# A graph-attention layer: one merged edge and one-hot product per group, a TensorE loop without register work, and a scratch write on Pool at every second group

## The chip, the cores and the metric

The kernel runs on one core of a Trainium2 chip. The metric is the device time of one execution, in microseconds (us); lower is better. Three runs of the kernel before gave 4992.13, 4989.86 and 4984.16 us, with a median of 4989.86 us.

## The reference

There are 12500 nodes with 128 features and 412500 edges with 64 features, sorted by their `dst`. Cut to what matters:

```python
h = x @ Wn + bn ; q = x @ Wq + bq ; k = x @ Wk + bk ; v = x @ Wv + bv
eh = edge_attr @ We + be
attn_in = concatenate([q[src], k[dst], eh], -1)          # per edge
hmid = leaky_relu(attn_in @ A1 + b1, 0.2)
scores = leaky_relu(hmid @ A2 + b2, 0.2)                 # 8 heads
w = softmax(scores.mean(-1), axis=0)                     # over all edges
out = segment_sum(w[:, None] * v[dst], src)
y = layernorm(h + out) * gamma + beta
result = layernorm(x + y)
```

## The kernel before

`attn_in @ A1` is split in three: a product of the source node, one of the destination node and one of the edge's features. The table phase (25 chunks of 512 nodes) computes the two node products for all nodes. The source products (`pq`) go to a table in memory (`pq_dram`). The destination products (`pk`) stay in the on-chip memory as a sum of three bf16 tables (high, middle, low), which ScalarE (L581, L586), VectorE (L811) and Pool (L495) make.

The main loop then goes over the edges in 403 pairs of groups; a group is 512 edges, so there are 806 groups. The weights of the softmax are needed only at the end, and nearly all of them are zero there, so the tail handles only tiles with weights above zero. In the main loop each group passes these steps:

- Pool gathers the source products of the group's edges with four indirect DMAs of 128 rows (L500), into one of 8 slots of `rows`. Before it gathers into a slot again, it waits until TensorE has used it (`s_added`, L514).
- SyncE loads `dst` and the edges' features of a pair (L402, L405), two pairs ahead of their use at most.
- VectorE compares `dst` with a window of 128 nodes, which gives a one-hot matrix in bf16 (L909).
- TensorE forms in one PSUM bank the product of the edges' features (fp32, L724), adds three bf16 products of the one-hot matrix with the three tables (L733), whose place in `pk` a register gives, and adds the gathered rows by four transposes (L713). A group whose edges cross into the next window of 128 nodes gets three more products (L744) in a loop behind an `If`.
- The last transpose raises `s_added`. ScalarE scales the bank (L612), VectorE takes the maximum (L926, the leaky relu), and TensorE multiplies the result by the head weights (L692, fp32). This product is called `score_mm`, and it stands behind the next group's products in TensorE's order.
- For every four groups ScalarE and VectorE apply the heads' leaky relu (L604, L933), TensorE transposes the heads (L700) and VectorE sums them to scores (L940).

In the first half of the main loop, each second pair also handles a block of 128 nodes: a product on TensorE (L763) and two layer norms on VectorE.

The order of the work on each engine is written out by hand in `pair_step` and `node_step` of each engine; `over_pairs` loops over them with four pairs in a turn. Where a step needs the number of its window or the count of further windows, its engine loads it from the table `info` into a register (`info_of`, L328) and works on it with register instructions (L731, L733, L736). TensorE's own piece of this for each group is

```python
word = word_of(pe, g)                                   # L729, one load per pair
first, more = window_of(word, h)                        # L730
pe.wait_ge(s_onehot, g + 1)
for c in range(3):                                      # L733
    pe.matmul(to, flat[:, bass.ds(first * (3 * P) + c * P, P)], onehot[:, h, :], ...)
with pe.If(more > 0): ...
```

Of the kernel before, what the change touches and what calls it, by code (L numbers as in the profile page):

```python
# [22 lines left out]
EXTRA = 1  # L43
QUAD = 4
SLOPE = 0.2
EPS = 1e-5
MORE = 256
# [4 lines left out]
FIRST_PAIRS = 3  # L52
FIRST = 2 * FIRST_PAIRS
TURN_PAIRS = 4
RING = 2 * TURN_PAIRS
SRC_RING = 4
# [6 lines left out]
def over_pairs(eng, pairs, blocks, pair_step, node_step):  # L63


    for q in range(FIRST_PAIRS):
        pair_step(q, q % 2, q // 2, None, 0)
    total = (pairs - FIRST_PAIRS) // TURN_PAIRS
    assert total * TURN_PAIRS + FIRST_PAIRS == pairs
    halves = TURN_PAIRS // 2  # L70
    with_nodes = -(-(blocks + BLOCK_LAG) // halves)
    peel = -(-BLOCK_LAG // halves)
    full = blocks // halves
    assert total > with_nodes + 1 and full > peel

    def iteration(i, nodes):
        for u in range(TURN_PAIRS):
            n = FIRST_PAIRS + u
            pair_step(n + TURN_PAIRS * i, n % 2, n // 2 + halves * i, u, i)
            if nodes:  # L80
                node_step(halves * i + u // 2, u % 2)

    for i in range(peel):
        iteration(i, True)
    with eng.Fori(peel, full) as i:
        iteration(i, True)
    for i in range(full, with_nodes):
        iteration(i, True)
    with eng.Fori(with_nodes, total - 1) as i:
        iteration(i, False)  # L90
    iteration(total - 1, False)
# [8 lines left out]
def build(nc, x_rows, x_blocks, x_chunks, edges, src_first, src_ring, dst_pairs, dst_spans, src_tiles, dst_tiles, wqT, wkT, weT, wv, wn,  # L100
          bn, bq, bk, bv, be, A1, b1, A2, b2, gamma, beta, out, n_edges):
# [9 lines left out]
    assert chunks * CW == n_pad and D == P and 2 * DE == P and tiles < KEY and blocks <= MORE and n_pad <= 1 << 16  # L111
    info_parts = P
    info_cols = dst_spans.shape[1] // GROUP
    turns = (pairs - FIRST_PAIRS) // TURN_PAIRS
    assert info_parts * info_cols >= groups and turns * TURN_PAIRS + FIRST_PAIRS == pairs
    assert (turns - SRC_RING) % SRC_RING == 0 and info_cols + 8 < chunks
# [3 lines left out]
    pq_dram = nc.dram_tensor("pq_dram", (n_pad, D), F32).ap()  # L120
    y_dram = nc.dram_tensor("y_dram", (n_pad + P, D), F32).ap()
# [1043 lines left out]
```

## Time and profile before

| | before |
|---|---|
| median of three runs | 4989.86 us |
| the profiled execution, its own time | 4998.4 us |
| its span, from the first to the last instruction | 4996.5 us |
| TensorE (PE) busy | 3236.5 us, 65% |
| Pool busy | 3095.7 us, 62% |
| VectorE (DVE) busy | 1407.0 us, 28% |
| ScalarE (ACT) busy | 736.6 us, 15% |
| mean granted TensorE clock | 0.798 of full speed |
| mean busy share of the 16 DMA engines | about a third in the main loop |

No engine is busy for more than two thirds of the span. A busy share doesn't tell what an engine waits for between its instructions; for that, the rows below show idle time with what ended it. "Remote" and "another core or an unknown queue" stand where the profile could not tie the end of a wait to a recorded instruction; with one core in use there is no other core. In a row of a group of instructions, the first number after the bar is the group's busy time, the second the mean duration of one in ns; after the second bar stands the idle time of the engine just before them.

### The profile page before, as it was taken

To read this page: it belongs to the slowest core of one execution; us is meant where nothing else is said; L and a number is where in the kernel's file an instruction comes from. 1 tells how busy PE (TensorE), PEld (TensorE's weight loads), DVE (VectorE), ACT (ScalarE), POOL (GpSimd) and SP (SyncE) were. 2 spreads that over 40 slices of the span, in tenths; PEclk is the share of its full clock that TensorE was granted. 3 is DMA by queue.
4 is the path that set the end of the run, shared out by engine and by line. 5 is a ranking of instruction groups with operands and counts; after the bars stand their busy time and mean duration, and the time that the engine had idled before them with its cause. 6 is when DMAs were issued, how large, how long until landed. Compare 5 with 4: busy or idle time off the path is not lost.

```text
span 4996.5 us, 58367 instructions
## 1 busy us (share of the span) xinstructions
PE 3236.5 (65%) x10213; PEld 1586.8 (32%) x10416; DVE 1407.0 (28%) x3449; ACT 736.6 (15%) x1268; POOL 3095.7 (62%) x3270
## 2 busy tenths in 40 slices
PE   5566666666666666676666666666666666666665
PEld 3233333333333333333333323333333332333332
DVE  4233333333333333333332222222222222222223
ACT  2111111111111111111111111111111111111111
POOL 5566666666666666666666666666666666666663
PEclk8788778788777878878788787877777788877787
DMA  5333333333333333333333333333333333333332
GB/s 159 88 98 98 98 96 100 97 98 99 96 100 96 97 96 102 96 96 100 98 96 89 88 85 90 89 88 87 90 85 86 90 87 88 88 86 88 88 88 60
DMA packets 311865, 467.39 MB, mean 94 GB/s; under 512 B 88001, under 2 KB 153665, under 8 KB 311698
## 3 DMA queue, kind: packets, MB, share of 16 engines
q1 hardware_dynamic: 207138, 254.92, 17.1%
q0 software_dynamic: 103328, 211.82, 16.3%
q10 hardware_dynamic: 1360, 0.20, 0.0%
q8 instruction: 15, 0.25, 0.0%
q14 instruction: 24, 0.20, 0.0%
HBM read 446.78 MB, written 19.86 MB: 93 GB/s over the span
## 4 chain that ended last, share of the span: by engine, by line
another core or an unknown queue 39%; PE 29%; issue 20%; ACT 5%; DVE 5%; DVEq 2%; ACTq 0%; DMA 0%; SPq 0%; POOL 0%; POOLq 0%
PE banks L692 9%; PE banks L724 7%; PE banks L733 5%; PE banks L713 5%; ACT sloped L612 3%; DVE hidden L926 3%; ACT head_s L604 1%; PE banks L744 1%; PE banks L700 1%; DVEq L328 1%; DVE onehot L909 0%; DVEq L97 0%; DVEq L909 0%; ACT node_m L621 0%
## 5 line engine op out<-in xcount | busy, mean ns | idle before, releaser
L500 POOL DMA_INDIRECT rows<-pq_dram,src_i x3200 | 3032.3, 948 | 1799.3 <-issue 929.9
L692 PE MATMUL banks<-hidden,a_wide 128*128 128x512 f32 x1612 | 1101.0, 772 | 1101.5 <-DVE hidden L926 1021.6
L926 DVE SCALAR_TENSOR_TENSOR hidden<-banks,bias_col,sloped 128x512 f32<-128x512 f32 x806 | 604.8, 750 | 2867.4 <-ACT sloped L612 2229.2
L612 ACT ACTIVATE sloped<-banks,bias_col 128x512 f32<-128x512 f32 x806 | 540.2, 686 | 4009.1 <-remote 2387.4
L724 PE MATMUL banks<-edge,w_fold 128*128 128x512 f32 x1612 | 1017.5, 719 | 42.8 <-issue 21.6
L733 PE MATMUL banks<-onehot,pk 128*128 128x512 bf16 x2216 | 714.9, 428 | 307.9 <-issue 187.6
L692 PEld LDWEIGHTS banks<-hidden,a_wide 128*128 128x128 f32 x1612 | 300.5, 233 | 1179.3 <-DVE hidden L926 1087.4
L713 PE MATMUL banks<-ident,rows 128*128 128x128 f32 x3224 | 551.8, 299 | 132.7 <-issue 131.4
L733 PEld LDWEIGHTS banks<-onehot,pk 128*128 x2418 | 264.5, 109 | 1039.0 <-issue 969.4
L713 PEld LDWEIGHTS banks<-ident,rows 128*128 128x128 f32 x3224 | 449.5, 157 | 347.3 <-issue 241.2
L724 PEld LDWEIGHTS banks<-edge,w_fold 128*128 128x128 f32 x1612 | 361.2, 236 | 442.3 <-issue 420.7
L909 DVE TENSOR_SCALAR onehot<-dst_b,iota_f 128x512 bf16<-128x512 uint16 x806 | 295.8, 367 | 80.0 <-issue 63.1
L744 PE MATMUL banks<-extra,pk 128*128 128x512 bf16 x291 | 101.2, 434 | 128.9 <-issue 114.2
L700 PEld LDWEIGHTS banks<-ident,head_l 128*128 128x128 f32 x808 | 126.2, 170 | 153.6 <-issue 151.8
L700 PE MATMUL banks<-ident,head_l 128*128 128x128 f32 x808 | 152.1, 322 | 2.8 <-issue 1.7
L933 DVE SCALAR_TENSOR_TENSOR head_l<-banks,b_cols,head_s 128x512 f32<-128x512 f32 x202 | 150.1, 743 | 7.7 <-issue 7.7
L604 ACT ACTIVATE head_s<-banks,b_cols 128x512 f32<-128x512 f32 x202 | 138.0, 683 | 2.7 <-PE banks L692 2.7
L940 DVE TENSOR_REDUCE score<-banks 128x128 f32 (+1 forms) x202 | 57.5, 285 | 267.3 <-remote 208.9
L744 PEld LDWEIGHTS banks<-extra,pk 128*128 x291 | 30.2, 104 | 192.2 <-issue 175.7
L621 ACT ACTIVATE node_m<-node_m,cols 128x1 f32<-128x1 f32 x200 | 58.4, 292 | 176.1 <-issue 120.4
L917 DVE TENSOR_SCALAR extra<-dst_b,iota_f 128x512 bf16<-128x512 uint16 x97 | 35.3, 364 | 167.6 <-issue 167.6
L658 PE MATMUL banks<-w_fold,xa 128*128 128x256 f32 x200 | 48.7, 397 | 10.4 <-DVE w_fold L803 5.1
(133 smaller groups left out, 630.5 us busy)
## 6 DMA issues: line engine op xcount, KB each, us to landing
dst_b<-in_dst_pairs_dram SPq DMA_DIRECT2D x403, 256.0 KB
edge<-in_edges_dram SPq DMA_DIRECT2D x403, 256.0 KB
rows<-pq_dram,src_i POOLq DMA_INDIRECT x3200
xa<-in_x_chunks_dram SPq DMA_DIRECT2D x25, 256.0 KB, 3.3
pq_dram<-rows SPq DMA_DIRECT2D x25, 256.0 KB, 3.0
node_x<-in_x_blocks_dram SPq DMA_DIRECT2D x100, 64.0 KB
node_r<-in_x_rows_dram SPq DMA_DIRECT2D x100, 64.0 KB
y_dram<-node_y SPq DMA_DIRECT2D x100, 64.0 KB
```

What stands on the lines that cost most here:

```text
L500: pool.indirect_dma_start(to, None, pq_dram, bass.IndirectOffsetOnAxis(at, 0)).then_inc(s, 16)
L604: act.activation(head_s[:, :], heads[slot], ACT.Identity, bias=b2_cols[:, 1:2], scale=SLOPE).then_inc(s_head_s, 1)
L612: act.activation(sloped[:, h, :], pre[2 * slot + h], ACT.Identity, bias=bias_col[:, 1:2], scale=SLOPE).then_inc(s_sloped, 1)
L692: pe.matmul(heads[slot], a2_wide[:, j, :], hidden[:, j, :], start=(j == 0), stop=(j == QUAD - 1 or last), skip_group_check=True).then_inc( ...
L700: last = pe.transpose(turned[:, k * P:(k + 1) * P], head_l[:, k * P:(k + 1) * P], ident[:, :])
L713: last = pe.matmul(pre[2 * slot + h][:, k * P:(k + 1) * P], four[k], ident[:, :], is_transpose=True, start=False, stop=(k == TILES - 1), s ...
L724: product = pe.matmul(to, w_fold[:, 2 + h, :], edge[:, slot, :], start=True, stop=False, skip_group_check=True)
L733: last = pe.matmul(to, flat[:, bass.ds(first * (3 * P) + c * P, P)], onehot[:, h, :], start=False, stop=False, skip_group_check=True)
L744: last = pe.matmul(to, flat[:, bass.ds(at, P)], extra[:, w, :], start=False, stop=False, skip_group_check=True)
L909: dve.tensor_scalar(onehot[:, h, :], dst, iota_f[:, bass.ds(first, 1)], None, ALU.is_equal).then_inc(s_onehot, 1)
L926: dve.scalar_tensor_tensor(out=hidden[:, j, :], in0=pre[j], scalar=bias_col[:, 0:1], in1=sloped[:, h, :], op0=ALU.add, op1=ALU.max).then_i ...
L933: dve.scalar_tensor_tensor(out=head_l[:, :], in0=heads[slot], scalar=b2_cols[:, 0:1], in1=head_s[:, :], op0=ALU.add, op1=ALU.max).then_inc ...
```

## The change

1. **Windows of 64 nodes from the pair's first `dst`.** The destination products stay in fp32 and are written to memory (`pk_dram`) in five pieces at the end of the table phase. For each pair SyncE loads the 64 rows of `pk_dram` that begin at the pair's lowest `dst` into the first 64 partitions of `window_w`, whose other 64 partitions hold the edge weights. The steps that made three bf16 tables are gone, Pool's L495 with them.
2. **One product.** VectorE writes the one-hot matrix as fp32 into the first 64 partitions of `moving` (one instruction of 1024 words for a pair); the edges' features are loaded into the other 64. One fp32 product of 128 rows per group gives both parts. The products of the former L733 and L744 are gone. Further windows are handled only if a pair spans more than 64 nodes.
3. **TensorE's loop.** The loop counter counts in steps of 64, and the semaphores that TensorE waits on count in the same steps, so that the waits compare with the counter itself. Buffers have fixed places. One load (the count of further windows in a turn) is left per turn of eight pairs, and one branch per pair.
4. **Order.** The pre-activation products of both groups of a pair come first, then both groups' transposes, then the head products of the pair before. ScalarE and VectorE work on both groups of a pair. Heads are collected over 16 groups in place of four.
5. **Pool.** The ring of gathered rows has 16 slots in place of 8. After every second group's gathers Pool writes 512 words per partition of the scratch tile `pace` (`pause`).
6. **SyncE.** It loads four pairs ahead, when `s_added` tells that the pair in the same slot is done.

The diff, cut to its core:

```diff
+TURN_PAIRS = 8
+PACE = 512
+PACED = 2
+RING = 2 * TURN_PAIRS
+AHEAD = 4
+SHOWN = 2
...
@@ SyncE
+            for k in range(PK_PARTS):
+                sp.wait_ge(s_pk, chunks // PK_PARTS * (k + 1))
+                sp.dma_start(pk_dram[...], pk_blocks[...]).then_inc(s_pk_out, 16)
...
+            sp.wait_ge(s_pk_out, 16 * PK_PARTS)
+            def pair_load(p, slot):
+                at = word(sp, base, p, n_pad - WINDOW)
+                sp.dma_start(window_w[0:WINDOW, slot, :], pk_dram[bass.ds(at, WINDOW), :]).then_inc(s_pair[slot], 16)
+                sp.dma_start(dst_b[:, slot, :],
+                             dst_pairs[bass.ds(p, 1), :].to_broadcast([WINDOW, PAIR])).then_inc(s_pair[slot], 16)
+                sp.dma_start(moving[WINDOW:P, 2 * slot:2 * slot + 2, :]..., edges[bass.ds(p, 1), :, :]...)
...
+                        sp.wait_ge(s_added, 2 * n + 2)
+                        pair_load(n + AHEAD, u % AHEAD)
@@ Pool
-            for c in range(chunks):
-                pool.wait_ge(s_pk_mid, c + 1)
-                pool.tensor_tensor(pk[..., 2, :], ..., ALU.subtract).then_inc(s_pk_lo, 1)
+            def pause(n):
+                wait(pool, s_paced, n)
+                pool.sem_inc(s_passed, 1)
+                pool.memset(pace[:, :], 0.0).then_inc(s_paced, 1)
             def turn(i, w, later, of=RING):
                 pool.wait_ge(s_src[w], ...)
                 for r in range(of):
                     if not isinstance(i, int) or i > 0:
-                        pool.wait_ge(s_added, FIRST + RING * i + r - RING + 1)
+                        pool.wait_ge(s_added, RING * i + r - RING + 1)
                         pool.sem_inc(s_passed, 1)
                     for k in range(TILES):
                         gather(rows[:, r, k, :], src_i[:, w, at:at + 1], s_rows[r])
+                    if r % PACED == PACED - 1:
+                        pause(RING // PACED * i + r // PACED)
@@ TensorE
+            def pair_step(u, tick):
+                first, slot = 2 * (u % 2), u % AHEAD
+                if u == 0:
+                    more[0] = word(pe, more_i, tick >> TICK_BITS, windows)
+                pe.wait_ge(s_onehot[u], tick)
+                for h in range(2):
+                    pe.matmul(pre[first + h], window_w[:, slot, :], moving[:, 2 * slot + h, :], start=True, ...)
+                with pe.If(more[0] > 0):
+                    ...
+                for h in range(2):
+                    pe.wait_ge(s_rows[2 * u + h], tick)
+                    for k in range(TILES):
+                        last = pe.matmul(pre[first + h][...], rows[:, 2 * u + h, k, :], ident[:, :], is_transpose=True, ...)
+                    last.then_inc(s_added, 1)
+                if u > 0:
+                    heads_of_pair(u - 1, tick)
...
+            def heads_of_pair(u, tick, last_pair=False):
+                pe.wait_ge(s_hidden[u], tick)
+                for h in range(2):
+                    last = pe.matmul(heads, a2_wide[:, 2 * u + h, :], hidden[:, 2 * (u % 2) + h, :], ...)
@@ VectorE
+            def show(p, slot, s, loaded):
+                dve.wait_ge(s_pair[slot], loaded)
+                dve.tensor_scalar(moving[0:WINDOW, 2 * slot:2 * slot + 2, :]...,
+                                  dst_b[:, slot, :], base_f[:, bass.ds(p, 1)], None, ALU.is_equal).then_inc(s, TICK)
```

## Rows read from the trace of the kernel before

**Rows 1.** From the page: busy us (share of the span) and instructions of each engine.
```profile
PE 3236.5 (65%) x10213; PEld 1586.8 (32%) x10416; DVE 1407.0 (28%) x3449; ACT 736.6 (15%) x1268; POOL 3095.7 (62%) x3270
```
**Rows 2.** The chain that ended last, by engine, from the page.
```profile
another core or an unknown queue 39%; PE 29%; issue 20%; ACT 5%; DVE 5%; DVEq 2%; ACTq 0%; DMA 0%; SPq 0%; POOL 0%; POOLq 0%
```
**Rows 3.** Waits: engine line, who ended them: us in total, times, longest.
```profile
ACT sloped L612 <- remote: 2387.4, 258, 28.1
ACT sloped L612 <- PE banks L713: 1050.1, 222, 14.4
...
POOL rows L500 <- remote: 721.9, 241, 3.9
...
POOL rows L500 <- PE banks L713: 147.5, 78, 4.4
```
**Rows 4.** Timeline of ScalarE from 85 to 175 us: start, duration, what, idle before.
```profile
128.68 0.69 ACT L612 ACTIVATE sloped<-banks,bias_col 128x512 f32<-128x512 f32 x1 [28.08 <-remote]
156.01 0.69 ACT L612 ACTIVATE sloped<-banks,bias_col 128x512 f32<-128x512 f32 x1 [26.64 <-remote]
```
**Rows 5.** Timeline of TensorE's products in the same stretch.
```profile
106.26 0.60 PE L713 MATMUL banks<-ident,rows 128*128 128x128 f32 x4
...
134.30 0.60 PE L713 MATMUL banks<-ident,rows 128*128 128x128 f32 x4
```
**Rows 6.** Timeline of Pool: first gather, end of the first run, last gather.
```profile
79.92 1.29 POOL L500 DMA_INDIRECT rows<-pq_dram,src  x1 [3.04 <-DMA pq_dram<-rows]
...
149.16 0.94 POOL L500 DMA_INDIRECT rows<-pq_dram,src_i  x1 [0.30 <-issue]
165.80 0.95 POOL L500 DMA_INDIRECT rows<-pq_dram,src_i  x1 [15.69 <-issue]
...
4940.79 0.95 POOL L500 DMA_INDIRECT rows<-pq_dram,src_i  x1 [0.30 <-issue]
```
**Rows 7.** Timeline from 4028 to 4050 us: one run of Pool, and ScalarE behind it.
```profile
4029.89 0.96 POOL L500 DMA_INDIRECT rows<-pq_dram,src_i  x1 [3.71 <-remote]
...
4038.57 0.60 PE L713 MATMUL banks<-ident,rows 128*128 128x128 f32 x4
...
4043.66 0.94 POOL L500 DMA_INDIRECT rows<-pq_dram,src_i  x1 [0.30 <-issue]
...
4047.21 0.69 ACT L612 ACTIVATE sloped<-banks,bias_col 128x512 f32<-128x512 f32 x1 [9.36 <-remote]
4047.96 0.94 POOL L500 DMA_INDIRECT rows<-pq_dram,src_i  x1 [3.35 <-remote]
```
**Rows 8.** Line L500, all gathers in the ring: duration ns min/median/max, first and last start.
```profile
L500 POOL DMA_INDIRECT rows<-pq_dram,src_i x3200: 941/947/1101, 110.4 to 4940.8; - x189
```
**Rows 9.** Pool's scratch and constant writes, from the groups by line.
```profile
L481 POOL MEMSET ones_f<- 128x128 f32 x1 | 0.2, 195 | 0.0
...
L483 POOL MEMSET ones_b<- 128x1 bf16 x1 | 0.1, 92 | 0.0
```
**Rows 10.** Chain from 157 to 163 us: start, us, what; half clock, then full clock.
```profile
157.54 2.08 PE banks L692 x2
...
162.22 0.86 PE banks L692 x2
163.08 0.86 PE banks L724 x2
163.94 0.65 PE banks L733 x3
164.59 0.44 PE banks L713 x4
```
**Rows 11.** Groups by line: ScalarE's scaling and VectorE's one-hot matrix.
```profile
L612 ACT ACTIVATE sloped<-banks,bias_col 128x512 f32<-128x512 f32 x806 | 540.2, 686 | 4009.1 <-remote 2387.4 <-PE banks L713 1050.1 <-issue 563.5
...
L909 DVE TENSOR_SCALAR onehot<-dst_b,iota_f 128x512 bf16<-128x512 uint16 x806 | 295.8, 367 | 80.0 <-issue 63.1 <-DMA dst_b<-in_dst_pairs_dram 9.8 <-remote 7.0
```
**Rows 12.** Line L733, TensorE's register instructions: duration ns min/median/max, first and last start.
```profile
L733 PEldq FUSED_REGOPS  x2418: 3/46/1419, 87.9 to 4954.5; - x186
```

More of the change, by code:

```diff
@@ L451, in _ @@
-            for j in range(full, with_nodes):
-                four_turns(j, True)
-            with sp.Fori(with_nodes, fours - 1) as j:
-                four_turns(j, False)
-            four_turns(fours - 1, False)
+            for p in range(AHEAD):
+                pair_load(p, p)
+            with_nodes = 1 - (-(blocks + BLOCK_LAG) // (TURN_PAIRS // 2))
+            full = blocks // (TURN_PAIRS // 2)
+            turn(0, 0, False)
+            turn(1, 1, True)
+            with sp.Fori(1, full // SRC_RING) as j:
+                two_turns(j, True)
@@ L458, in _ @@
+            after = full // SRC_RING * SRC_RING
+            ends = -(-with_nodes // SRC_RING) * SRC_RING
+            for i in range(after, ends):
+                turn(i, i % SRC_RING, i < with_nodes)
+            with sp.Fori(ends // SRC_RING, turns // SRC_RING - 1) as j:
+                two_turns(j, False)
+            for i in range(turns - SRC_RING, turns):
+                turn(i, i % SRC_RING, False)
             sp.wait_ge(s_left, 1)
@@ L684, in _ @@
+            pe.wait_ge(s_window_e, 1)
+            pe.wait_ge(s_info, INFO)
             pe.sem_inc(s_extra_used, 1)
[L685 to L693 removed]
@@ L695, in heads_turn @@
-            def heads_turn(quad):
-                pe.wait_ge(s_head_l, quad + 1)
-                wait(pe, s_score, quad)
+            more = [None]
+            def heads_of_pair(u, tick, last_pair=False):
+                pe.wait_ge(s_hidden[u], tick)
+                if u == 0:
+                    pe.wait_ge(s_head_l, tick)
+                for h in range(2):
+                    g = 2 * u + h
+                    ends = g == RING - 1 or (last_pair and h == 1)
+                    last = pe.matmul(heads, a2_wide[:, g, :], hidden[:, 2 * (u % 2) + h, :], start=(g == 0), stop=ends,
+                                     skip_group_check=True)
+                    if ends:
+                        last.then_inc(s_heads, 1)
@@ L701, in heads_turn @@
                 last.then_inc(s_head_t, 1)
-            def add_rows(q, h, slot, u, i):
-                g = 2 * q + h
-                if isinstance(q, int) and q < FIRST_PAIRS:
-                    pe.wait_ge(s_rows_0[g], 64)
-                    four = [rows_0[:, g, k, :] for k in range(TILES)]
-                else:
-                    pe.wait_ge(s_rows[2 * u + h], 64 * (i + 1))
-                    four = [rows[:, 2 * u + h, k, :] for k in range(TILES)]
-                for k in range(TILES):
-                    last = pe.matmul(pre[2 * slot + h][:, k * P:(k + 1) * P], four[k], ident[:, :], is_transpose=True,
-                                     start=False, stop=(k == TILES - 1), skip_group_check=True)
-                last.then_inc(s_added, 1)
@@ new lines, in relu, with heads_relu @@
+            def relu(g, j, s):
+                dve.wait_ge(s_sloped, g + 1)
+                last = dve.scalar_tensor_tensor(out=hidden[:, j, :], in0=pre[j], scalar=bias_col[:, 0:1],
+                                                in1=sloped[:, j, :], op0=ALU.add, op1=ALU.max)
+                if s is not None:
+                    last.then_inc(s, TICK)
+            def heads_relu(batch):
+                dve.wait_ge(s_head_s, batch + 1)
+                dve.scalar_tensor_tensor(out=head_l, in0=heads, scalar=b2_cols[:, 0:1], in1=head_s, op0=ALU.add,
+                                         op1=ALU.max).then_inc(s_head_l, TICK)
```

712 lines of the change are left out of this document (329 added, 383 removed).

## The prediction, made before the changed kernel ran

> **What bounds the kernel now.** I read the busy shares first: no engine passes 65%, Pool has 62% [rows 1]. So the end is set by waits, and the chain that ended last says the same: 39% of it is a wait whose end the profile can't name, more than TensorE's own 29% [rows 2]. The list of waits says who stands in it: ScalarE waits 2387.4 + 1050.1 us for the bank that TensorE fills, and Pool waits 721.9 + 147.5 us in 319 stalls for slots of its ring [rows 3]. Both wait for one signal, `s_added`, raised by the last transpose of a group.
>
> The timeline shows that this signal comes late. TensorE's transposes of one group are recorded at 106.26 and end by 106.9; ScalarE, with nothing before it, starts on a bank only at 128.68. The transposes at 134.30 end by 134.9; the next start is at 156.01 [rows 4, 5]. Waits of 28.08 and 26.64 us, while TensorE does nothing that is recorded. What is special about this stretch is Pool: from 79.92 to 149.16 it issues 56 gathers without a gap above 0.3 us, then it has a full ring and stands still until 165.80 [rows 6]. After its stop the next signal comes within 6 us. In steady work the same is seen smaller: Pool issues 12 gathers from 4029.89 to 4043.66; transposes are recorded at 4038.57, but ScalarE starts only at 4047.21, after 9.36 us of idling and 2.6 us after Pool's last gather ended (4043.66 + 0.94 = 4044.60); Pool itself then stalls 3.35 us for the same signal [rows 7]. I read this as: while Pool issues gathers without a break, TensorE's signals are held back; Pool fills its ring, stops, and the signals pass. This reading is a correlation of rows. The other candidate is TensorE's own register work: three register instructions per group at L733 with a median of 46 ns but up to 1419 ns [rows 12].
>
> Pool is therefore the clock of the main loop, with stalls on top. One gather takes 947 ns (941 to 1101) [rows 8] and the next starts 0.30 us later [rows 6], so 1.25 us each. 806 groups x 4 = 3224 gathers x 1.25 = 4030 us. From the first gather to the end of the last, 4941.7 - 79.9 = 4861.8 us passed [rows 6]. The difference, 832 us, is stalls. This is all that a change which keeps the gathers can win in that stretch.
>
> **The change part by part.**
>
> *Products.* At full clock a group's parts on TensorE take 0.86 (head product), 0.86 (edges), 0.65 (three one-hot products) and 0.44 us (transposes) [rows 10]. The 0.65 goes; the merged product has the shape of the edge product and costs the same 0.86. Per pair that is 2 x 2.16 = 4.3 us at full clock; at half clock some 8.7 us, since one head product there takes 2.08 us with its start [rows 10] and I double the rest. Both lie under Pool's 10.0 us per pair, so this part is worth nothing by itself. It gives slack: 1.3 us per pair at full clock, and the group loops at L744 go.
>
> *TensorE's register work and order.* Before, each group is one round: signal, ScalarE 0.69 us [rows 11], VectorE, head product. After, a pair is one round, and its head products stand behind the next pair's products and transposes (2.6 us), which hide ScalarE's and VectorE's work. Register instructions fall away but for one load per eight pairs. Below: nothing; above: the whole 832 us, if they hold the signals. Either reading puts the gain in the same 832 us, so I count it once.
>
> *Pool's write.* 128 words take 195 ns and one word 92 ns [rows 9]: 0.81 ns a word, so 512 words take 0.51 us. The trace has no such write between gathers. Low end: it fills the 0.30 us between two gathers and costs 0.2. High end: it has such a gap on either side, 1.1. I take 0.65 us (the write and half a gap), nearest to the measured write. 403 x 0.65 = 262 us (81 to 443). In return Pool's runs are cut to 8 gathers, 10 us, where before they are 12 to 56. Waiting for the earlier write (`s_paced`) costs nothing: that is eight gathers old.
>
> *The ring of 16* lets Pool be up to 80 us ahead, so a late signal of 10 us no longer stops it, unless TensorE falls behind on average.
>
> *Table phase.* Pool's, ScalarE's and VectorE's extra passes go, the span reductions stay and a load and eight short steps move ahead; before, the first gather is at 79.92. I leave it there (70 to 90). SyncE stores 6.4 MB of destination products before the first pair is loaded, which delays TensorE, not Pool: its ring takes 64 gathers, 80 us, until it must wait. For the case that this cover is short I add one stall as at 165.80, about 20 us.
>
> *VectorE.* One write of 1024 words per pair in place of two of 367 ns [rows 11], 0.7 to 1.4 us, with two relus and the node work well under 10 us per pair; hidden. *SyncE* issues three loads and one register load per pair, four pairs (40 us) ahead; hidden.
>
> A rule speaks against this part. The Trainium skill ("SBUF — State Buffer", section "SBUF: two separate sides") says that VectorE in a two-port mode and GpSimd lock each other out of a shared port pair for a whole instruction, and that descriptors for Pool's DMAs can't be written meanwhile. In this trace the longest of 3200 gathers is 1101 ns against a median of 947 ns [rows 8] beside 806 one-hot writes [rows 11], so at most 0.15 us of it is seen.
>
> **The sum.** 79.9 + 4030 + 262 + 20 + what follows the last gather, 4998.4 - 4941.7 = 56.7 (the last groups, softmax and the tail, nearly unchanged) = 4449 us on the profiled execution's time of 4998.4. The median of the runs shown is 8.5 us lower, so 4440 us.
>
> **Rivals.**
>
> *A: half of it.* The signals still come late, and the pair's one round decides: 4861.8 / 403 = 12.06 us per pair now, less 1.3 us of products and plus 0.65 for the write = 11.4 us; 403 x 11.4 + 137 - 8.5 = 4720 us. For it: nothing in the trace shows that 0.5 us is break enough; holds end about 2.6 us after a run does [rows 7]. Against: half the rounds, twice the ring.
>
> *B: slower.* The write doesn't break Pool's run as far as the signals are concerned; only a stop of some microseconds does. Then the stalls stay, since the larger ring only postpones them, and each write lengthens the stream that sets the time: 4990 + 262 = 5250 us. It decides from the point at which more than 832 - 262 = 570 us of stalls are left. For it: each release in rows 4, 6 and 7 but that of 128.68 follows a real stop. Against: 8 gathers are shorter than the run of 12 before the hold in rows 7.
>
> *C: VectorE locks Pool.* If each one-hot write stopped Pool for its whole length, 2 x 367 ns, 403 x 0.73 = 296 us come on top: 4735 us. The 1101 ns speaks against it. This is the rule named above.
>
> *D: no change*, where the stalls fall by just what the writes cost: 4990.
>
> *E: better*, the writes cost 0.2 and the table phase is 10 us shorter: 4440 - 181 - 30 = 4230.
>
> **How the numbers follow.** Forecast 0.62, A 0.18, B 0.11, C 0.05, D 0.02, E 0.02. The forecast's own range is 4270 to 4620, from the ends of the write's price. To hold the time 8 times in 10 I take 4270 to 4880, which takes in A and C and leaves out B, most of D, and E. A measurement of this kernel tells about 0.2% from no change; faster 0.87, within it 0.02, slower 0.11.
>
> **What would show it.** Right: Pool's gathers at 1.25 us with one write after every eighth, under 100 us of stalls, a pair every 10.6 us; ScalarE's waits of 20 us and more gone; TensorE ending some 16 us after the last gather as now. Wrong: Pool stalls of 3 us in number with waits of 8 to 10 us before ScalarE (A, B); gathers longer than 1.1 us (C); a write that takes 1 us or more with its gaps (the price). If a pair takes 10.6 us and the ring is never full, the write itself is what bounds, beside the gathers.

## The result, and the profile after

| | median | from to | ratio to before, 95% interval |
|---|---|---|---|
| before, beside it | 4989.7 us | 4984.2 to 4992.1 | |
| after | 5128.4 us | 5111.5 to 5149.2 | 1.028 (1.024 to 1.032) |

The changed kernel is 2.8% slower; 4440 us was forecast. From the page of the kernel after: its span, the busy time of each engine, the granted clock in 40 slices (tenths of full speed), and the chain that ended last.

```profile
span 5132.7 us, 37113 instructions
...
PE 2366.8 (46%) x7100; PEld 1219.7 (24%) x7101; DVE 1251.8 (24%) x2609; ACT 634.3 (12%) x1093; POOL 3331.3 (65%) x3666
...
PEclk8676776777677767777777776767677677767677
...
another core or an unknown queue 38%; issue 26%; SPq 18%; PE 12%; DVE 2%; ACT 1%; DMA 1%; ACTq 0%; DVEq 0%; POOL 0%; POOLq 0%
```

TensorE has 870 us less to do than in [rows 1], and it gained nothing: no engine is above 65%, and the unnamed wait still leads the chain with 38% [rows 2]. SyncE's queue is new in it, with 18%. The granted clock is 0.72 in the mean (0.80 before): (1 - 0.722) / 0.5 = 56% of the time at the lower of its two levels, with TensorE idle for more than half of the span.

The waits of the kernel after: engine, tile and line, who ended them, us in total, times, longest.

```profile
ACT pk_sb L610 <- remote: 2617.3, 244, 33.2
...
PE banks L746 <- DMA node_x<-in_x_blocks_dram: 453.4, 55, 21.8
ACT pk_sb L610 <- PE banks L729: 440.9, 94, 26.6
...
POOL rows L496 <- DMA src_i<-in_src_ring_dram: 343.3, 36, 13.1
POOL rows L496 <- remote: 243.2, 89, 6.0
...
POOL rows L496 <- PE banks L729: 180.3, 42, 13.3
```

ScalarE's unnamed waits, 2387 us before [rows 3], are 2617 us now, and the longest grew from 28 to 33 us. Pool still stalls: 343.3 + 243.2 + 180.3 = 766.8 us in 167 stalls, 717 us beyond the usual gap of 0.30; the same count over [rows 3] gives 869.4 - 319 x 0.30 = 774 us. The forecast's 832 us also hold the gaps that are a little over 0.30; with those the kernel after has 754 us. The stalls are fewer and longer, and the largest part waits for the list of indices (`src_i`), which SyncE loads only once the same late signal has passed.

The timeline of the kernel after from 4021 to 4052 us (start, duration, engine, what, idle before). It is the stretch that answers to [rows 7].

```profile
4021.17 0.95 POOL L496 DMA_INDIRECT rows<-pq_dram,src_i  x1 [0.17 <-POOL pace L502]
...
4026.66 0.71 SPq L394 DMA_DIRECT2D window_w<-pk_dram  x1
...
4027.52 1.04 PE L729 MATMUL banks<-ident,rows 128*128 128x128 f32 x8
...
4030.91 0.70 SPq L395 DMA_DIRECT2D pk_sb<-in_dst_pairs_dram  x1
4030.94 0.55 POOL L502 MEMSET pace<- 128x512 f32 x1
4031.66 0.95 POOL L496 DMA_INDIRECT rows<-pq_dram,src_i  x1 [0.17 <-issue]
...
4035.16 0.70 SPq L397 DMA_DIRECT2D pk_sb<-in_edges_dram  x1
...
4041.38 0.54 POOL L502 MEMSET pace<- 128x512 f32 x1
4045.03 1.27 ACT L610 ACTIVATE pk_sb<-banks,bias_col 128x512 f32<-128x512 f32 x2 [21.96 <-remote]
...
4045.89 0.48 SPq L394 DMA_DIRECT2D window_w<-pk_dram  x1
...
4046.55 0.47 SPq L395 DMA_DIRECT2D pk_sb<-in_dst_pairs_dram  x1
...
4047.87 0.43 SPq L340 DMA_DIRECT2D src_i<-in_src_ring_dram  x1
...
4051.75 0.95 POOL L496 DMA_INDIRECT rows<-pq_dram,src_i  x1 [9.83 <-DMA src_i<-in_src_ring_dram]
```

This one view shows most of it. TensorE's transposes of 4027.52 are done by 4028.6. Pool goes on issuing gathers, with writes at 4030.94 and 4041.38 among them, and nothing passes at the write of 4030.94. After the last write Pool has nothing to do (it needs the next indices); 3.1 us after that write's end ScalarE starts, on signals some 16 us old. (It then handles four groups in a row; by count, two of them were transposed by 4022.8 and had waited 22 us.) The trace also records when a semaphore rises: for `s_added` four rises stand at 4045.01 to 4045.28, and none between 4022.36 and those. So it is the signal that is late, and not ScalarE. SyncE is slowed too: its three loads of one pair have no wait between them, and are issued 4.25 us apart (4026.66, 4030.91, 4035.16) while Pool streams, 0.66 us apart after it has stopped (4045.89, 4046.55). Over the whole trace they are 1.5 us apart in the median, and 3.6 us or more in one case of ten, while Pool streams, and 0.67 us outside. Its load of indices comes last of all, at 4047.87, and Pool waits 9.83 us for it.

### The profile page after: what moved, and what is told of

Same layout as the page of the kernel before. It is cut to its first block, busy times and chain, and to the rows that moved or that the text cites. A ratio compares the mean times of both kernels' runs of the same rounds, so it can differ in the third digit from the quotient of the medians.

```text
span 5132.7 us, 37113 instructions
## 1 busy us (share of the span) xinstructions
PE 2366.8 (46%) x7100; PEld 1219.7 (24%) x7101; DVE 1251.8 (24%) x2609; ACT 634.3 (12%) x1093; POOL 3331.3 (65%) x3666
## 4 chain that ended last, share of the span: by engine, by line
another core or an unknown queue 38%; issue 26%; SPq 18%; PE 12%; DVE 2%; ACT 1%; DMA 1%; ACTq 0%; DVEq 0%; POOL 0%; POOLq 0%
PE banks L692 5%; PE banks L712 4%; SPq L324 3%; SPq L394 3%; SPq L395 3%; SPq L397 3%; PE banks L729 2%; ACT pk_sb L610 1%; SPq L403 1%; SPq L415 1%; SPq L85 1%; SPq L407 1%; SPq L411 1%; SPq L423 1%
## 5 line engine op out<-in xcount | busy, mean ns | idle before, releaser
L692 PE MATMUL banks<-pk_sb,a_wide 128*128 128x512 f32 x1612 | 1010.6, 760 | 1941.5 <-DVE pk_sb L887 909.2
L887 DVE SCALAR_TENSOR_TENSOR pk_sb<-banks,bias_col,pk_sb 128x512 f32<-128x512 f32 x806 | 581.4, 747 | 3550.4 <-ACT pk_sb L610 2880.1
L610 ACT ACTIVATE pk_sb<-banks,bias_col 128x512 f32<-128x512 f32 x806 | 524.3, 686 | 3589.3 <-remote 2617.3
L712 PE MATMUL banks<-pk_sb,window_w 128*128 128x512 f32 x1612 | 923.9, 703 | 40.6 <-issue 40.6
L692 PEld LDWEIGHTS banks<-pk_sb,a_wide 128*128 128x128 f32 x1612 | 340.0, 234 | 2283.8 <-issue 1323.4
L729 PE MATMUL banks<-ident,rows 128*128 128x128 f32 x3224 | 453.2, 284 | 74.6 <-issue 74.4
L712 PEld LDWEIGHTS banks<-pk_sb,window_w 128*128 128x128 f32 x1612 | 368.2, 236 | 479.8 <-issue 479.8
L746 PE MATMUL banks<-wn_sb,node_x 128*128 128x128 f32 x200 | 67.8, 434 | 658.0 <-DMA node_x<-in_x_blocks_dram 453.4
L870 DVE TENSOR_SCALAR pk_sb<-pk_sb,base_f 64x1024 f32<-64x1024 uint16 x403 | 304.3, 755 | 39.2 <-issue 39.1
L502 POOL MEMSET pace<- 128x512 f32 x403 | 223.2, 554 | 0.1
```

Source lines behind the costliest of these rows:

```text
L502: pool.memset(pace[:, :], 0.0).then_inc(s_paced, 1)
L610: act.activation(sloped[:, 2 * (u % 2) + h, :], pre[2 * (u % 2) + h], ACT.Identity, bias=bias_col[:, 1:2], scale=SLOPE).then_inc(s_sloped, 1)
L692: last = pe.matmul(heads, a2_wide[:, g, :], hidden[:, 2 * (u % 2) + h, :], start=(g == 0), stop=ends, skip_group_check=True)
L712: pe.matmul(pre[first + h], window_w[:, slot, :], moving[:, 2 * slot + h, :], start=True, stop=False, skip_group_check=True)
L729: last = pe.matmul(pre[first + h][:, k * P:(k + 1) * P], rows[:, 2 * u + h, k, :], ident[:, :], is_transpose=True, start=False, stop=(k == ...
L870: dve.tensor_scalar(moving[0:WINDOW, 2 * slot:2 * slot + 2, :].rearrange("p s n -> p (s n)"), dst_b[:, slot, :], base_f[:, bass.ds(p, 1)], ...
```

## Experiments

Each run stands beside runs of the kernel before on its own chip. These showed something that has to be known first: in some sets no signal is held at all, in either kernel, and the kernel before then takes 4160 us in place of 4990. The chip is not what decides: sets b and d ran on the same one. So each ratio is read within its set. Of the kernel before one trace is kept, that of the result; for it the last column goes by its time in the set, and for the other kernels by the traces of the set.

| set | before | signals held |
|---|---|---|
| result | 4989.7 | yes |
| a | 4934.3 | yes |
| b | 4995.0 | yes |
| c | 4163.1 | no |
| d | 4159.3 | no |
| e | 5002.3 | yes |

How late the signals are can be counted in each trace, from the recorded end of a group's last transpose to the start of ScalarE's instruction on that group (806 groups):

| run | median | longest | groups over 1.5 us |
|---|---|---|---|
| before | 3.3 us | 49 us | 477 |
| after | 8.4 us | 66 us | 584 |
| a1, no write | 9.6 us | 65 us | 573 |
| a2, stop after 8 gathers | 0.04 us | 2.4 us | 1 |
| a3, a quarter of the gathers | 0.5 us | 3.8 us | 176 |
| a4, lead 4 | 7.5 us | 20 us | 586 |
| b1, stop after 16 | 10.5 us | 55 us | 617 |
| b2, four writes after 8 | 0.04 us | 4.6 us | 2 |
| b3, three more signals | 8.9 us | 63 us | 566 |
| b4, lead 8 | 9.6 us | 32 us | 624 |
| e1, other one-hot, lead 8 | 9.3 us | 39 us | 616 |
| e2, two writes after 8 | 12.1 us | 49 us | 698 |
| every run of c and d | 0.04 us | 0.2 us | 0 |

From ScalarE's instruction to VectorE's on the same group it is 0.10 us in the median in the kernel after, in a1 and in c1 alike, and over 1.5 us 4 times, 3 times and never. The delay is on what TensorE's matmuls raise, and not on signals in general.

The theories: **H**, that TensorE's signals wait until Pool issues no gather for long enough, and **L**, that Pool is innocent and TensorE's rounds and SyncE's loads make the waits.

**a1: without the write.**
```
-                    if r % PACED == PACED - 1:
-                        pause(RING // PACED * i + r // PACED)
```


> The kernel after, with Pool's 512-word write and its wait taken out; nothing else differs. Theory H (TensorE's signals are held back while Pool issues gathers in an unbroken stream, and a write is no break in it): holds of 20 to 33 us before ScalarE stay; Pool's stream loses 403 x 0.41 us = 167 us, so about 4960 us, or up to 5130 where the holds grow by what the stream gains. Theory W (the write does break the stream, and something else makes the kernel slow): without the write the holds become longer and more, 5300 us or above. Theory P (the write itself is the damage): under 4800 us, with the waits of ScalarE above 15 us gone.

Measured: 5087.5 us, ratio 1.031 (1.029 to 1.033); ScalarE's longest unnamed wait 37.2 us. The holds stay, as H has it, and P (the write is the damage) falls. W (the write breaks the stream) has little left: the longest wait grew by 4 us, the time did not grow. So the write was neither the damage nor much of a help: the kernel after has 1.028 against its own before. Whether its small price shows at all where signals are held is not told apart by ratios of two sets.

**a2: a real stop after every 8 gathers, no write.**
```
-                        pause(RING // PACED * i + r // PACED)
+                        pool.wait_ge(s_rows[r], 16 * TILES * (i + 1))
+                        pool.sem_inc(s_passed, 1)
```


> The kernel after, with a real stop of Pool in place of the write: after every second group (8 gathers) Pool waits until that group's gathers have landed, which I put at 2 to 3 us. Theory H: signals pass in each stop, so ScalarE's waits above 15 us vanish and Pool never waits for its ring; a pair takes 10.0 + 2.5 to 3 us, 403 x 12.5 to 13 + 137 = 5180 to 5380 us, all of it gathers and stops. Theory L (the loads of SyncE and the order of TensorE's rounds make the waits, Pool is innocent): the waits before ScalarE stay at 20 us and more and Pool's stalls of some 650 us come on top of the stops, 5700 us and above.

Measured: 5184.7 us, ratio 1.051 (1.049 to 1.053). Its waits:

```profile
ACT pk_sb L611 <- PE banks L730: 3012.6, 637, 7.2
...
POOL rows L496 <- DMA rows<-pq_dram,src_i: 800.6, 324, 7.1
```

One unnamed wait of 0.7 us is left of 2617, none before ScalarE in the loop is over 7.2 us, and the stops make the time: eight gathers of 0.98 us in the mean, seven gaps of 0.32 and one of 2.5 are 12.57 us a pair; 403 pairs and the 124 us before the first gather and behind the last give 5190 us. The waits are now TensorE's own for rows to land. L falls, and Pool's stream is what matters. H as worded isn't the whole of it, though: signals do not wait here for the next stop, they are not late at any point of the eight gathers. In the kernel before, too, of the rises recorded for matmuls that ended within 6 us of the start of a run of gathers 73 of 686 come over 1.5 us late, of the later ones 1321 of 1532. The stop costs more than it gives back, because it comes at every pair.

**a3: a quarter of the gathers, no write.**
```
-                    for k in range(TILES):
+                    for k in range(1):
...
-                    pe.wait_ge(s_rows[2 * u + h], tick)
+                    pe.wait_ge(s_rows[2 * u + h], tick >> 2)
```


> The kernel after without the write and with three of four gathers left out (TensorE adds the first tile's rows four times, so the output is another one). Pool's part is 1.25 us per group. Theory H: TensorE runs at its own pace, some 8 to 9 us per pair with no hold above 5 us: 403 x 8.5 + 137 = 3560 us, 3100 to 3700. Theory L: the waits of 20 us before ScalarE come from TensorE's rounds and SyncE's loads and stay: 4600 us and above.

Measured: 2080.7 us. From the page, busy times and the chain:

```profile
PE 1878.4 (91%) x7100; PEld 1036.3 (50%) x7101; DVE 1233.9 (60%) x2609; ACT 621.4 (30%) x1093; POOL 788.0 (38%) x845
...
PEclk9699999999999999999999999999999999999996
...
PE 56%; issue 16%; DVE 13%; ACT 5%; SPq 3%; DMA 3%; another core or an unknown queue 1%; DVEq 1%; ACTq 1%; POOL 0%; POOLq 0%
```

Faster than both theories had it: TensorE is 91% busy and the granted clock is 0.977, where H reckoned with a pair of 8.5 us; (2072 - 137) / 403 = 4.8 us per pair. The new loop of TensorE, with SyncE's loads behind it, can do a pair in less than half of Pool's 10 us at the higher clock. That it is not the bound at the clock of the kernel after either is shown by c1 below, where Pool never waits for it. The run leaves out three quarters of the transfers too, so by itself it doesn't tell Pool's issuing from the traffic.

**a4 and b4: Pool at most 4, or 8, groups ahead, no write.** The ring keeps its 16 slots; 8 is the lead of the kernel before.
```
-                    if not isinstance(i, int) or i > 0:
-                        pool.wait_ge(s_added, RING * i + r - RING + 1)
+                    if not isinstance(i, int) or RING * i + r >= LEAD:
+                        pool.wait_ge(s_added, RING * i + r - LEAD + 1)
...
-                    if r % PACED == PACED - 1:
-                        pause(RING // PACED * i + r // PACED)
```


> The kernel after without the write; the ring keeps its 16 slots, but Pool may be only 4 groups ahead of TensorE's signals, so its unbroken runs end after 16 gathers (20 us) at the latest and mostly earlier. Theory H: the short lead makes the stops that let signals pass, holds are at most 20 us and mostly 10: 4850 to 5050 us, faster than the kernel after. Theory D (depth of the ring is what saves Pool from a late signal): less lead, more stalls, 5250 us and above.

> The kernel after without the write, and Pool at most 8 groups ahead, which is the ring of the kernel before. Theory H (a deeper lead lets Pool stream longer before it must stop, and nothing else): between the 4843 us of a lead of 4 and the 5088 us of 16, 4900 to 5000. If the lead does not matter and 4 was won otherwise: 5080 us. If the merged loop alone, at the lead of the kernel before, is what makes it slower: 5100 us and above.

Measured: lead 4, 4842.8 us, ratio 0.982 (0.980 to 0.983); lead 8, 4879.3 us, ratio 0.977 (0.975 to 0.978); lead 16 was 1.031. By these ratios both are faster than both kernels of the case. The waits with a lead of 8:

```profile
ACT pk_sb L609 <- remote: 2283.9, 242, 25.6
...
POOL rows L497 <- remote: 558.7, 154, 6.5
...
POOL rows L497 <- PE banks L728: 129.9, 43, 6.2
```

Pool stalls for 689 us, in nearly two hundred short stops of which none is over 6.5 us, and `src_i` is no longer among them. b4 came out 21 us below the range expected of it, a4 7 us. So what is left of the change without the write and the deeper lead (the merged product, the order, the earlier loads) is worth 2.3% where signals are held, and the lead of 16 takes 5.5% away (1.031 / 0.977). That figure is from two sets; within set a, a1 takes 5.1% longer than a4.

**b1: the stop of a2 after every 16 gathers.**

> The stop of the run before (Pool waits until its last gathers have landed, 2.1 us longer than the usual gap) after every 16 gathers in place of every 8, no write. Theory H (signals wait for a stop of Pool): one stop in 22.2 us. If both pairs of such a stretch get through (one early in the stream, one in the stop) Pool's stream and stops set the time: 202 x 22.2 + 137 = 4620 us, up to 4750. If a stop lets only one pair through, Pool's ring fills and the stalls come back: 5000 us and above.

Measured: 5012.2 us (4978 to 5042), ratio 1.002 (0.999 to 1.005), and ScalarE's unnamed waits are back, 331 of them, up to 25.5 us. This is the expectation's second case; that each stop lets just one pair through was not counted.

**b2: four writes in a row after every 8 gathers.**
```
-                        pause(RING // PACED * i + r // PACED)
+                        for k in range(4):
+                            pause(4 * (RING // PACED * i + r // PACED) + k)
```


> The kernel after with four 512-word writes in a row after every 8 gathers in place of one, each waiting for the one before it: Pool issues no gather for some 2.2 to 2.8 us, as long as in the stop of 2.1 us that let all signals pass, but it is busy in them. Theory G (it is the stream of gathers that holds signals, and only its gap counts, idle or not): as with the stop, no wait of ScalarE above 10 us, 403 x (10.0 + 2.5) + 137 = 5180 us, 5130 to 5350. Theory I (Pool must be idle or waiting): the waits stay at 20 us and more and the writes come on top: 5128 + 403 x 1.7 = 5800 us.

Measured: 5306.6 us, ratio 1.062 (1.060 to 1.064). Its waits, and Pool in its timeline:

```profile
ACT pk_sb L611 <- PE banks L730: 3198.7, 646, 42.3
```
```profile
4009.99 0.95 POOL L496 DMA_INDIRECT rows<-pq_dram,src_i  x1 [0.31 <-issue]
4010.93 0.54 POOL L502 MEMSET pace<- 128x512 f32 x1
4011.63 0.53 POOL L502 MEMSET pace<- 128x512 f32 x1 [0.15 <-POOL pace L502]
4012.31 0.53 POOL L502 MEMSET pace<- 128x512 f32 x1 [0.15 <-POOL pace L502]
...
4012.98 0.53 POOL L502 MEMSET pace<- 128x512 f32 x1 [0.15 <-POOL pace L502]
4013.63 0.69 ACT L611 ACTIVATE pk_sb<-banks,bias_col 128x512 f32<-128x512 f32 x1 [3.99 <-PE banks L730]
4013.80 0.95 POOL L496 DMA_INDIRECT rows<-pq_dram,src_i  x1 [0.29 <-PE banks L730]
```

One unnamed wait of 5.2 us is left (the named one of 42.3 us is the loop's first, for the loads behind the table phase; the longest after it is 10.4 us). Pool is busy with writes, and signals pass all the same. A busy Pool does not hold them (G, and not I); with 2.9 us without a gather after every eighth (4010.94 to 4013.80) none is late.

**b3: three more signals of TensorE behind each group.**

> The kernel after without the write, and TensorE raises another semaphore three times after each group's last transpose. Theory Q (a held signal leaves when the next one of the same engine comes behind it): holds shrink, under 4700 us. Theory H (signals of TensorE wait until Pool stops, whatever follows them): within 1.5% of the 5088 us without the write. If every signal costs time of its own, more.

Measured: 5128.7 us, ratio 1.026 (1.024 to 1.028); holds up to 38.8 us. Theory Q falls: what follows a held signal does not push it out. The three signals themselves come from TensorE's sequencer and not from a matmul, and are not late: the trace has 838 of their rises, 0.01 us in the median behind the instruction, two of them over 1.5 us. TensorE as a whole is therefore not cut off; what comes late is the word that a matmul is done.

**c1 and c2: the kernel after, and the same without the write.**

> The kernel after as it is, beside the next run on the same chip: the ratio to the kernel before should be the 1.028 of the result, within 0.5%.

> The kernel after without the write, again, to price the write against the kernel after on one chip. If the write costs what its stream shows (403 x 0.41 us = 167 us) and does nothing else, this is 3.3% faster than the kernel after. If Pool has slack in its stalls and the write only fills it: within 0.5%. If the write does let some signals pass: slower than the kernel after.

Measured: 4401.8 us, ratio 1.058 (1.056 to 1.059), and 4250.0 us, ratio 1.021 (1.020 to 1.023). The expectation of c1 fell at once: no signal is held here. The chain of the kernel after, and its waits:

```profile
POOL 63%; issue 28%; DMA 5%; PE 2%; POOLq 1%; DVE 1%; SPq 0%; ACT 0%; DVEq 0%
```
```profile
ACT pk_sb L610 <- PE banks L729: 2909.8, 801, 43.5
...
POOL rows L496 <- issue: 858.5, 2816, 0.3
POOL rows L496 <- POOL pace L502: 66.1, 402, 0.2
```

Pool never waits for its ring and sets the time, as the forecast had it, and this time of 4402 us is the forecast's sum within 1%. That is in part luck: the write costs about 110 us less than was reckoned and no stall of 20 us came, and gathers grew longer by 87 us, which the sum had at nothing. And the kernel before has lost its stalls as well. What is left is what the change adds to Pool: the write, 4401.8 - 4250.0 = 152 us, and 87 us (4250.0 - 4163.1) without it. Those are in the gathers. The groups by line of c2, and one gather beside VectorE's one-hot write:

```profile
L496 POOL DMA_INDIRECT rows<-pq_dram,src_i x3224 | 3141.1, 974 | 1038.8 <-issue 982.5 <-DMA pq_dram<-rows 56.3
```
```profile
3013.51 0.74 DVE L868 TENSOR_SCALAR pk_sb<-pk_sb,base_f 64x1024 f32<-64x1024 uint16 x1
...
3013.69 1.37 POOL L496 DMA_INDIRECT rows<-pq_dram,src_i  x1 [0.30 <-issue]
```

974 ns in the mean against a median of 947 before [rows 8]: 3224 x 0.027 = 87 us. Over the whole trace, the 457 gathers that overlap this write take 1148 ns, the others 946.

**c3 and c4: a write after every 4 gathers; two writes after every 8.**
```
-PACED = 2
+PACED = 1
```
```
-                        pause(RING // PACED * i + r // PACED)
+                        for k in range(2):
+                            pause(2 * (RING // PACED * i + r // PACED) + k)
```


> One 512-word write after every 4 gathers instead of every 8. Theory R (a write starts a new stream, and streams of 5 us hold nothing): Pool sets the time, 4030 + 806 x 0.41 + 137 = 4500 us. Theory S (a gap in the gathers has to be long, and 0.5 us is not): the holds stay, 5100 to 5300 us.

> Two 512-word writes in a row after every 8 gathers, some 1.25 us that Pool issues no gather beyond the usual gap (one write: 0.41 us; four: 2.57 us, which let all signals pass). If 1.25 us is enough: 403 x (10.0 + 1.25) + 137 = 4680 us, 4650 to 4800. If it is too short: the holds stay and the writes lengthen the stream, 5100 to 5450 us.

Measured: 4592.1 us, ratio 1.103 (1.102 to 1.105), and 4767.0 us, ratio 1.146 (1.144 to 1.147). With nothing held they price the writes and tell nothing of their effect: 403 more writes cost 190 us when each stands alone, 365 us as second of two.

**d1: the kernel before with the write alone.**
```
+                    if r % 2 == 1:
+                        wait(pool, s_paced, RING // 2 * i + r // 2)
+                        pool.sem_inc(s_passed, 1)
+                        pool.memset(pace[:, :], 0.0).then_inc(s_paced, 1)
```


> The kernel before with the 512-word write after every second group alone. Where signals are held: a write of 0.41 us is no break; the stalls of the kernel before (832 us) can take some of it up, so between the same time and 403 x 0.41 = 167 us more, ratio 1.00 to 1.034. If the write does break the stream: under 0.95. Where no signal is held: Pool sets the time and the whole 167 us come on top, ratio 1.04.

Measured: 4324.3 us, ratio 1.040 (1.038 to 1.042), 165 us more, within 2 us of the 167 expected. No signal was held.

**d2, d3 and d4: b4, c3 and c4 again,** to have them where signals are held, which failed.

> The kernel after without the write, Pool at most 8 groups ahead. Where signals are held: 0.977 of the kernel before, as on the chip before. Where none is: the lead does not matter, the ratio is the 1.021 that the lead of 16 had.

> One write after every 4 gathers. Where signals are held: theory R (a write starts a new stream, and streams of 5 us hold nothing) says Pool sets the time, 4500 to 4600 us, ratio 0.91 to 0.93; theory S (0.5 us is too short a gap) says the holds stay, ratio 1.02 to 1.06. Where none is held: 1.10 again.

> Two writes after every 8 gathers, a gap of 1.4 us more than usual. Where signals are held: if the gap is enough, 4765 us as on the chip without holds, ratio 0.95 to 0.96; if too short, 5150 to 5450 us, ratio 1.03 to 1.09. Where none is held: 1.145 again.

Measured: 4250.3, 4587.5 and 4763.0 us, ratios 1.022, 1.103 and 1.145. The lead of 8 and that of 16 (c2) are equal here, so the lead matters only through the holds. On the same chip, b4 was 4879 us: 629 us between one kernel with and without held signals.

**e1: the one-hot as a scalar_tensor_tensor with a tile of ones; lead 8, no write.**
```
-                dve.tensor_scalar(... dst_b[:, slot, :], base_f[:, bass.ds(p, 1)], None, ALU.is_equal)
+                dve.scalar_tensor_tensor(... in0=dst_b[:, slot, :], scalar=base_f[:, bass.ds(p, 1)], in1=ones_w[:, :],
+                                         op0=ALU.is_equal, op1=ALU.mult)
```


> The kernel with a lead of 8 and no write, and VectorE makes the one-hot as a scalar_tensor_tensor with a tile of ones in place of the tensor_scalar; gathers beside the tensor_scalar took 1148 us per thousand, others 946. Theory V (that form of VectorE's write blocks Pool's gathers): gathers beside it fall to 950 ns, and where no signal is held the time is 4250 - 403 x 0.2 = 4170 us, ratio 1.000 to 1.005 in place of 1.022. Theory M (the traffic to the shared rows of memory lengthens them, whatever the form): the gathers stay long, ratio 1.02 to 1.03. Where signals are held: 0.975 to 0.98 either way, since Pool has stalls to absorb it.

Measured: 4881.8 us, ratio 0.976 (0.975 to 0.977). Groups by line:

```profile
L497 POOL DMA_INDIRECT rows<-pq_dram,src_i x3224 | 3182.5, 987 | 1618.3 <-issue 944.6 <-remote 550.8 <-PE banks L728 66.0
...
L870 DVE SCALAR_TENSOR_TENSOR pk_sb<-pk_sb,base_f,ones_w 64x1024 f32<-64x1024 uint16 x403 | 511.4, 1269 | 43.0 <-DMA pk_sb<-in_edges_dram 38.5 <-issue 4.4
```

The gathers did not fall to 950 ns but rose to 987 in the mean (b4: 959), those beside the write take 1124 (1148 beside the other form in c2), and the write is longer, 1269 ns, so that it touches more of them: 739 in place of 522 in b4. Theory V in this form falls; the time does not move, since Pool's stalls took it up. The result repeats b4's ratio in another set.

**e2: two writes after every 8 gathers, signals held at last.**

> Two writes after every 8 gathers. Where signals are held: if the gap of 1.4 us more than usual is enough, Pool sets the time, 4765 us, ratio 0.95 to 0.96; if too short, 5150 to 5450 us, ratio 1.03 to 1.09. Where none is held: 1.145.

Measured: 4981.6 us (4960.6 to 4996.3), ratio 0.996 (0.994 to 0.997), between the two expectations:

```profile
ACT pk_sb L611 <- remote: 2567.0, 397, 28.4
...
POOL rows L496 <- DMA src_i<-in_src_ring_dram: 151.7, 22, 9.7
POOL rows L496 <- remote: 68.9, 58, 3.1
...
POOL rows L496 <- PE banks L730: 44.5, 22, 9.0
```

The signals are as late as ever (12.1 us in the median), but Pool stalls for 265 us in place of 767. I counted in both traces where ScalarE's waits above 8 us before its scaling end: within 1.5 us behind the end of a write or a pair of writes, 10 of 147 in the kernel after, 47 of 175 here. That stretch is about an eighth of the time in both, so two writes in a row let some signals pass; one lets next to none.

## Why the prediction was wrong

**The step that failed** is that of Pool's write: "In return Pool's runs are cut to 8 gathers, 10 us". A write of 0.55 us, a gap of 0.7 us between two gathers, cuts nothing as far as the signals are concerned (4030.94 above): ScalarE's longest unnamed wait is 33 us with it and 37 without (a1), and 754 us of the 832 us of stalls and gaps are left. Four in a row do cut (b2), two do so in part (e2). Rival B had named this mechanism, with the point from which it decides, 570 us of stalls left; 717 were left. It had 0.11. Its price of 5250 us is 122 too high: the write cost 165 in place of 262 and the stalls and gaps fell by 78, while longer gathers took back 42 and the two ends some 7. The sum of the kernel after: 73.3 to the first gather + 4030 + 165 for the write + 42 for longer gathers (961 ns in the mean) + 717 + 68.4 behind the last gather = 5096; the rest of the 5132.7, 37 us, are gaps slightly longer than usual.

**The ring.** Its part, that "a late signal of 10 us no longer stops it", failed too: the signals did not stay at 10 us. Where Pool's stream holds them, a longer lead lets Pool go on longer: between two stalls the median stream is 12 gathers before and 24 after, and one group in ten waits over 32 us (a1) where it is 23 us with a lead of 8 (b4) and 15 with 4 (a4). This is the larger loss, 5.5% between b4 and a1, and it was costed at nothing.

**The reading of the profile was right in the main.** Pool's stream of gathers goes with TensorE's late signals (a2, b2), though not every signal waits for a stop: of the late rises 147 of 1478 in the kernel before, and 168 of 553 in the kernel after, are recorded while Pool goes on, as the one behind 128.68 in [rows 4] is. And a stream alone is not enough, since in c and d it holds nothing. Pool's stream bounds the loop, and the stalls are what a change can win: without holds the kernel before takes 4163 and 4159 us, and the same sum without write and stall, 79.9 + 4030 + 56.7 - 8.5, gives 4158.

**The register work** was put beside the stream as second candidate. The new loop has almost none and its signals are held as before, so it was not the cause. **The products** were right: hidden, 4.8 us per pair at the higher clock (a3) for an estimate of 4.3. What they save can be no more than the 2.3% of b4, and in c and d it is nothing.

**The write's price** was taken too high, 0.65 us for a measured 0.41 (d1): it starts right when the gather ends, and the next gather follows after 0.17 us, so that write and gap take 0.71 us in place of the usual 0.30. The high end of 1.1 us counted the usual gap as a cost.

**Two slips in the sums** changed nothing. A pair at half clock comes to 2 x (2.08 + 1.72 + 0.88) = 9.4 us by the prediction's own terms and not 8.7, still under Pool's 10.0; and the low end of the forecast's range is 4440 - 181 = 4259, not 4270.

**Rival C** was right in kind and too high in price: 87 us (c2), and 42 in the kernel after, in place of 296. The row of 1101 ns [rows 8] showed two short writes of bf16 per pair; the new one is twice as long, and gathers beside it reach 1477 ns. The gather above is longer by 0.42 us where it overlaps the write for 0.56. The Trainium skill ("SBUF — State Buffer", section "SBUF: two separate sides") also names a VectorE instruction with two SBUF inputs as one that takes the shared port pair, against a GpSimd instruction that reads SBUF. The form chosen in e1 has two such inputs, and gathers beside it are longer too (1124 ns, at most 2004). That fits the rule if a gather counts as such an instruction, which no run here shows. Gathers beside the form with one input are longer as well (1148 ns in c2), and about a third of them (149 of 457) are not longer at all, so the runs don't tell a lock of the ports from another cause; a form with neither property was not tried.

**SyncE** was called hidden. It is not, since it waits for `s_added` too, and its own issues are slow in a stream where signals are held: 343 us of Pool's stalls wait for `src_i` with a ring of two, and TensorE waits 453 us for `node_x`. Neither is the root. Both vanish from Pool's and TensorE's waits where no signal is held (c1).

**Not settled:** what in the chip holds the signals, and why in some sets and not in others on one chip. Whether it is Pool's issuing or the transfers that it starts: the stop of a2 ends when the last rows have landed, 2.5 us behind the last gather, and the gap of b2 is as long. Whether a matmul's signal or its completion is late, since the profile models a matmul's end. Why at the same lead of 8 the signals of b4 are later (9.6 us) than those of the kernel before (3.3 us). What a single write does to the time where signals are held (1.028 with it and 1.031 without, from two sets). The kernel before with a deeper ring was not tried.

## What to carry to other kernels

Where a signal arrives only after its neighbour engine pauses, ask of each buffer made deeper whether it takes that pause away: here the lead of 16 cost 5.5%, and the plain merged loop with the lead of 8 beat both kernels (0.977, and 0.976 again), but only where signals are held; elsewhere none of the kernels beat the one before (1.021 at best). A pause has to be tried at the length that works before it is made cheap, and its price stands against what it frees. Work taken from an engine that mostly waits is worth little (870 us less on TensorE, 2.3% at most), and work added to the engine that streams counts in full once the stalls are gone.

## What the runs showed of the hardware

- The signals of TensorE's matmuls come late while Pool issues indirect gathers in a long stream: 8.4 us in the median and up to 66 us from a group's last transpose to ScalarE (the kernel after), with single waits of ScalarE up to 37 us (a1) and 39 us (b3). ScalarE's signals to VectorE (0.10 us) and those of TensorE's sequencer (0.01 us, b3) do not.
- With no gather for 2.5 us after every eighth, in which Pool waits (a2), or 2.9 us, in which it writes (b2), no signal of the loop is late. A gap of 1.5 us lets some through (e2), one of 0.7 us nearly none (each from the end of a gather to the start of the next).
- SyncE's DMA issues without a wait between them are 1.5 us apart in the median in such a stream, at most some 4 us, and 0.67 us outside (the kernel after). In a2, b2, c and d they are 0.54 to 0.65 us apart in the median.
- The effect is absent in some sets of runs: a stream of 3224 gathers (c2) then holds nothing, and the kernel with a lead of 8 takes 4250 in place of 4879 us on the same chip.
- A gather of 947 ns takes 1148 ns in the mean beside a VectorE write of 64 x 1024 fp32, at most 1477 ns (c2).
